# Weights written along the columns by ScalarE ahead of VectorE's multiply, in the joint stage of a graph network

## The reference, cut to what matters

```python
edge_index = jnp.stack([src, dst])
x = _layernorm(x + _L0_gnn_ref(x, edge_index, edge_attr_64, ...), axis=-1)
x = _layernorm(x + _L1_gnn_ref(x, edge_index, ..., 6250), axis=-1)
x = _layernorm(x + _L2_gnn_ref(x, edge_index, ...), axis=-1)
x = _layernorm(x + _L3_gnn_ref(x, edge_index, edge_weight, ...), axis=-1)

# in _L0: messages = relu(concat([x[src], edge_attr]) @ W1.T + b1) @ W2.T + b2
#         agg = segment_sum(messages, dst)
# in _L1, _L2: norm = dis[src] * dis[dst];       segment_sum(x[src] * norm, dst)
# in _L3:      norm = dinv[src] * w * dinv[dst]; segment_sum((x @ W)[src] * norm, dst), three times
```

## Time and profile before

| | |
|---|---|
| median of 3 runs | 5592.74 us (5584.71 to 5594.79) |
| the profiled execution's own time | 5637.0 us |
| its span | 5635.2 us |
| PE, DVE, ACT, POOL busy, share of the span | 85%, 44%, 21%, 21% |
| joint stage, from the first eviction to the last | 134 to 2080 us |
| granted TensorE clock, mean | 0.91 |

### The profile page before, as it was taken

One profiled execution on the slowest core, in us unless ns is written; L12 is line 12 of the kernel. 1 busy time (PEld: TensorE's weight loads), 2 busy tenths in 40 slices (PEclk: granted clock), 3 DMA queues, 4 the chain that ended last, 5 costly groups with the idle time before them and its releaser, 6 DMA issues. The chain is left out here.

```text
span 5635.2 us, 75975 instructions
## 1 busy us (share of the span) xinstructions
PE 4813.6 (85%) x30664; PEld 3047.7 (54%) x30664; DVE 2493.0 (44%) x4225; ACT 1157.3 (21%) x2219; POOL 1199.1 (21%) x845
## 2 busy tenths in 40 slices
PE   3788888888888863388879989999999999999999
PEld 2777777777777753233334444444444444454444
DVE  5877888888788767755542220111000000001111
ACT  0555555555555541100000000000000000000000
POOL 2655656566666610000000000000000000000000
PEclk6888988889898876689989999999999999999999
DMA  4665666666666651288876658887444444338887
GB/s 139 204 199 188 218 198 202 205 202 216 199 213 213 201 179 55 94 299 294 298 225 206 212 187 305 305 306 263 150 155 144 147 149 155 140 132 289 310 306 261
DMA packets 689173, 1178.49 MB, mean 209 GB/s; under 512 B 77284, under 2 KB 450384, under 8 KB 688440
## 3 DMA queue, kind: packets, MB, share of 16 engines
q1 hardware_dynamic: 617004, 1079.58, 55.6%
q0 software_dynamic: 26864, 55.10, 3.9%
q10 hardware_dynamic: 44956, 38.94, 2.2%
HBM read 823.64 MB, written 349.75 MB: 208 GB/s over the span
## 5 line engine op out<-in xcount | busy, mean ns | idle before, releaser
L756 POOL DMA_INDIRECT x<-p_table,src_i x832 | 1191.9, 1433 | 801.6 <-DVE x L553 516.3
L1197 PE MATMUL po_l3b<-mat_l3b,rows_b 128*128 128x512 f32 (+1 forms) x2548 | 1042.5, 569 | 12.2 <-DMA mat_l3b<-weights_fwd 12.2
L740 ACT CAST st_cnt<-ps_mat 128x512 bf16<-128x512 f32 x1225 | 661.2, 585 | 749.4 <-PE ps_deg L665 373.4
L1197 PEld LDWEIGHTS po_l3b<-mat_l3b,rows_b 128*128 128x128 f32 x2548 | 467.6, 191 | 555.7 <-issue 542.4
L675 PE MATMUL ps_mat<-rows_a,hot_s 128*128 128x128 bf16 x7203 | 593.0, 240 | 100.1 <-issue 45.9
L660 PE MATMUL ps_mat<-rows_a,hot_s 128*128 128x128 bf16 x2401 | 396.5, 231 | 230.1 <-issue 81.4
L675 PEld LDWEIGHTS ps_mat<-rows_a,hot_s 128*128 128x128 bf16 x7203 | 482.5, 109 | 162.9 <-ACT st_wt L744 83.2
L1197 PE MATMUL po_l<-mat_l,rows_a 128*128 128x512 bf16 (+1 forms) x1911 | 429.6, 387 | 152.2 <-DVE mat_l L1365 152.2
L541 DVE TENSOR_TENSOR rows_a<-rows_a,slots 128x1536 bf16<-128x1536 bf16 (+1 forms) x294 | 543.5, 1885 | 2.4 <-issue 0.2
L1197 PE MATMUL po_l3a<-mat_l3a,rows_a 128*128 128x512 f32 (+1 forms) x1274 | 523.5, 570 | 16.2 <-DMA mat_l3a<-weights_fwd 16.2
L1197 PE MATMUL po_l3c<-mat_l3c,rows_a 128*128 128x512 f32 (+1 forms) x1274 | 522.1, 569 | 11.8 <-DMA mat_l3c<-weights_fwd 11.7
(11 more groups left out here) (334 smaller groups left out, 4777.3 us busy)
## 6 DMA issues: line engine op xcount, KB each, us to landing
weights_fwd<-st_wt SPq DMA_DIRECT2D x588, 256.0 KB
mat_l<-counts_fwd SPq DMA_DIRECT2D x168, 896.0 KB, 5.4
mat_l3a<-weights_fwd SPq DMA_DIRECT2D x84, 1792.0 KB, 7.1
mat_l3b<-weights_fwd SPq DMA_DIRECT2D x84, 1792.0 KB, 7.1
mat_l3c<-weights_fwd SPq DMA_DIRECT2D x84, 1792.0 KB, 7.1
counts_fwd<-st_cnt SPq DMA_DIRECT2D x588, 128.0 KB
counts_rev<-st_cnt SPq DMA_DIRECT2D x588, 128.0 KB
rev_l<-counts_rev SPq DMA_DIRECT2D x84, 896.0 KB, 7.9
```

The lines of the kernel that those rows point to most:

```text
L740: nc.scalar.copy(st_cnt[:, q, :, j * 2 * P:j * 2 * P + n_col], ps_mat[:, f % 3, :].rearrange("p (d c) -> p d c", d=2)[:, :, 0:n_col]).then ...
L756: pool.indirect_dma_start(ring[:, j % RING, t * FD:(t + 1) * FD], None, p_table, bass.IndirectOffsetOnAxis(src_i[:, j * TH + t:j * TH + t ...
L1197: mm = nc.tensor.matmul(po[:, g % 2, k, 0:nb * P].rearrange("p (d c) -> p d c", c=P), rows[:, s, k * P:(k + 1) * P], mat[:, n % slots, 0:n ...
```

## The change

A new semaphore `spread_w` counts planes. ACT gets a function `weights_along(u, h, v)`: it waits until the unit's slots are there and the half's one-hots of the unit before are used up, and copies plane v of the weights, read with step 0, along the 128 columns of each pair into `hot_w`, which is 128 x 1792 elements for the first half and 128 x 1536 for the second. DVE waits for the plane and multiplies it in place by `hot_d`. On ACT the copies for (u, 1) stand ahead of the evictions of blocks 1, 2 and 3 of unit u, those for (u+1, 0) ahead of the evictions of blocks 9, 10 and 11 of unit u, and those of (0, 0) ahead of everything in the stage.

```diff
@@ one_hots, DVE @@
                         dve.wait_ge(hot_d_ready, m + 1)
                         for v in range(3):
-                            V.tensor_tensor(hot_w[:, h, v, 0:n, :], hot_d[:, h, 0:n, :],
-                                            per_row(slots[:, u % 2, 2 + v, ks], P), ALU.mult).then_inc(hots_ready, 1)
+
+                            dve.wait_ge(spread_w, 3 * m + v + 1)
+                            V.tensor_tensor(hot_w[:, h, v, 0:n, :], hot_w[:, h, v, 0:n, :], hot_d[:, h, 0:n, :],
+                                            ALU.mult).then_inc(hots_ready, 1)
                             tick()
@@ the stage's block of ACT @@
+                    def weights_along(u, h, v):
+                        n = 2 * HALF if h == 0 else NK + 1 - 2 * HALF
+                        act.wait_ge(slots_ready, 2 * u + 1)
+                        if u:
+                            act.wait_ge(filled, (u - 1) * FILLS + (3 * HALF if h == 0 else FILLS))
+                        nc.scalar.copy(hot_w[:, h, v, 0:n, :], per_row(slots[:, u % 2, 2 + v, 2 * HALF * h:2 * HALF * h + n], P)
+                                       ).then_inc(spread_w, 1)
+
+                    for v in range(3):
+                        weights_along(0, 0, v)
                     for n in range(UN):
                         (u, s), q = divmod(n, SUBS), n % STAGES
                         w = sub_cols(s)
+
+                        if 1 <= s <= 3:
+                            weights_along(u, 1, s - 1)
+                        if 9 <= s <= 11 and u + 1 < NB:
+                            weights_along(u + 1, 0, s - 9)
                         for j, k in enumerate(sub_pairs(s)):
```

More of the change, by code:

```diff
@@ L412, in build @@
             sorted_, sort_read, slots_ready = sem("sorted"), sem("sort_read"), sem("slots_ready")
-            hot_d_ready, source_ready = sem("hot_d_ready"), sem("source_ready")
+            hot_d_ready, source_ready, spread_w = sem("hot_d_ready"), sem("source_ready"), sem("spread_w")
             hots_ready, filled, evicted = sem("hots_ready"), sem("filled"), sem("evicted")
```

## The result

The changed kernel takes 5812.7 us (median of 4 runs, 5803.7 to 5813.8) against 5593.8 us for the one before (4 runs, 5584.7 to 5605.1): a ratio of 1.0387, 95% interval 1.0365 to 1.0408. It is 219 us slower. What follows of the traces is about those 167 us.

The account below looks back on a forecast made before the run. No engine is full, so waits decide: PE waits for DVE's one-hots and ACT's evictions. First half -7, second half +88, clock +40 give +121 us: median 5592.7 to 5714 us; own range 5640 to 5810, 8 in 10 5560 to 5840.

Parts of the forecast that it names:

- the second half's terms: Blocks 9 to 11: ACT's copies overshoot its idle time by 1.8 us a unit, +88 us; clock term +40 us.
- the first half's: Up to the 8th block: 14 units start it 1.2 us later, 35 start it 0.7 us earlier, -7 us.
- The operations: DVE's multiplies fall to 1093 and 960 ns; ACT's six planes a unit take 1616 and 1410 ns, 418 us in all.
- Who pays for ACT's time: ACT's copies ahead of evictions in blocks 1 to 3 and 9 to 11 overshoot idle time by 1.2 and 1.8 us.
- rival (a): Joint stage: ACT's idle time absorbs the planes, leaving DVE's gain of about 60 us, 5533 us; chance 0.20.
- rival (c): DVE's multiply does not get faster, so DVE sets the 8th block as before: +145 us, 5738 us; chance 0.10.
- The gain at the 8th block: Start of a unit's second half: PE's waits for DVE's one-hots shrink, worth 65 us at most.
- that same slack: DVE's idle time before L494, waiting for ranks, 5.0 us a unit; message sums slide a few us inside it.
- The clock: Joint stage's granted clock falls from 0.87 to 0.84, PE's 1607 us grow by 57 us, 40 us taken.
- Rival (b): Joint stage: ACT's idle time is no cover, each copy counts in full, 353 us, 5946 us; chance 0.07.
- The rule on multiplies: Skill page's rule putting elementwise multiplies on VectorE, not ScalarE; taken as speaking against the change, with no number.

Follow-up runs that it names:

- e1_old_multiply: Changed kernel with ScalarE's planes kept, but VectorE overwrites them by the old step-0 multiply: 5807 us, 1.0331 of the kernel before.
- e2_no_planes: Kernel before with a dense multiply of the one-hots by themselves, no planes, weights left out: 5709 us, 1.0153 of before.
- e6: Kernel before with no planes and each dense multiply of the one-hots by themselves made twice: 5602 us, 0.9969 of before.
- e8: Kernel before with a dense multiply, no planes, weights left out and GpSimd's gathers left out: 5175 us, 0.9205 of before with gathers.
- e7: Kernel before with GpSimd's gathers left out, their semaphores counted up at once: 5374 us, 0.9557 of before with gathers.
- e9: Changed kernel with GpSimd's gathers left out, their semaphores counted up at once: 5479 us, 1.0163 of the kernel before with its gathers.
- third set: Three runs on one chip, kernel before 5388 us there: changed kernel without gathers (1.0163), kernel before with paced gathers (0.9996), changed kernel with paced gathers (1.0223).
- e12_pause_paced: Kernel before with only the second half's planes, ahead of block 0, dense multiply in that half, gathers paced: 5535 us, 0.9872 of before.
- e5_ranks_pause: Kernel before with only the second half's planes, all three ahead of block 0, dense multiply in that half: 5680 us, 1.0114 of before.
- e10_before_paced: Kernel before with each gather held back until a given number of PE's fills is evicted: 5388 us, 0.9996 of before.
- e11_after_paced: Changed kernel with each gather held back until a given number of PE's fills is evicted: 5518 us, 1.0223 of before.

## Why the prediction was right, and where its sum was not

Slower was right, and so was the range (5560 to 5840 us). The forecast was 121 us and the change cost 219; the forecast's own range, 5640 to 5810, is missed by 3 us. By the parts of a unit, clock included, the first half (blocks 0 to 6) grew by 47 us where the sum had -7, and the second with the ranks by 129 us where it had 88 and 40 for the clock. So the second half's terms came out, and the first half's failed, as far as the clock's share in each can be left aside.

- *The operations.* The multiplies fell as worked out. The planes were 84 and 91 ns longer each: 25 us in all, which the range held and the sum didn't.
- *Who pays for ACT's time.* Right in kind: idle time used up, PE waiting at evictions, rival (a) out. In size the two stretches of planes grew by 2.2 and 0.8 us where I had 1.2 and 1.8, nearly the sum that I gave them; that the errors cancel is luck. For the planes without any gain of VectorE's the sum is that of rival (c), 145 us, and e1_old_multiply cost 1.0331, 185 us on 5594.
- *The gain at the 8th block.* This step failed. The prediction counted DVE's head start as worth up to 65 us on the path and set it against the first half ("14 x 1.2 - 35 x 0.67 = -7 us"), which makes it worth 24 us in the sum (145 - 121). In the changed kernel it is worth nothing (e1_old_multiply; 219 us against 185, across chips, it even costs 34), and alone it costs 86 us (e2_no_planes). Part of the 65 us was misread as well: the 14.2 us behind L533 stand in blocks 8 and 9, where PE already had the half's one-hots. The wait itself did go, as foreseen; its time came back in blocks 7 and 8, 1.3 us a unit longer: PE's idle time in them grew by 43 us, its waits behind evictions of counts most of all, and its clock fell from 0.83 to 0.78. Late fills are in the changed kernel not what grew there: with first evictions they are 159 us in these two blocks before and 154 after (203 in e2_no_planes).
- *What an early engine sets off.* I had written of the message sums that "they slide by a few us inside that same slack" and looked at them as something that could come late. What they did by coming early, and what POOL did by running faster, I didn't price. The sign stood in the trace of before: ACT's 182 us of "remote" waits, and 127 us of PE's waits without a releaser, of which I named 81.4 (the other 45.9 are at L675). I priced neither. Most of the change's loss is the planes'; but this is what turned the expected gain round: VectorE early costs 86 us with gathers (e2), nothing once its time is given back (e6), and gains 199 us without gathers (e8 against e7).
- *The clock.* I took 0.84 and it was 0.84, but of the 57 us that this gives I counted 40 as visible; PE's busy time rose by 108 us. Why by more than the mean clocks give is not shown.
- *Rival (b)*, each plane in full, was nearer to the truth where nothing else disturbs: 304 us between e8 and e9 (across two chips, for 407 us more work of ACT), against its 353.
- *The rule on multiplies.* I took a rule that multiplies belong on VectorE as speaking against the change. The change leaves the multiplies on VectorE and gives ScalarE copies, so it doesn't bear on it.

Open: why fills come late. The runs show that it is PE's signal that is late, that it takes gathers (none without them, e7 and e8, on a chip that took 5620 us with them), that it isn't the gathers alone (none on the chip of the third set), and that dense gathers and late fills go together in time. Leaving the gathers out takes away GpSimd's instructions, their transfers and the waits of POOL and VectorE on each other at once; no run parts these. That the gathers' pitch is the cause was argued, and e12_pause_paced speaks against it as the whole cause. By what path an early VectorE makes more fills late, through GpSimd's gathers or through its own message sums, is argued too. Whether place or pacing makes e12's gain is also open, since no run had the one without the other on its chip.

## What to carry to other kernels

Before moving work between engines, ask of the engine that is relieved what it will release sooner, and into what; here 250 us less work on VectorE cost 86 us. Work put in front of evictions is largely paid when PE has only three banks between itself and them, whatever the engine's idle share over the stage says: 304 us for 407 us of work, where nothing else disturbed. Whether it is cheaper where PE does something that needs no eviction is a fair thing to try; e5_ranks_pause leaves it open. Read "remote" and unnamed waits against the times at which the semaphore was counted up, before pricing anything that stands near them. And take away a suspect (here the gathers) early, in both kernels: it told more than five variants of the change.

## What the runs showed of the hardware that I had not expected

- PE's semaphore updates can come up to 6 us after the last matmul of the fill (6.2 us in the example), in nine of the eleven traces with indirect gathers, and in none of the three without them. The two others, e10_before_paced and e11_after_paced, come from one chip: there the kernel before took 5388 us, and 5594 to 5625 us in the four other sets of runs.
- A GpSimd gather of 128 rows takes 0.94 us while VectorE does nothing and 1.84 us beside its two-input operations; the average over the stage is 1.43 us before and 1.19 us after, with shorter multiplies.
- A bf16 multiply with one operand at step 0 takes 2018 ns for 1792 columns, the dense one in place 1095 ns; a ScalarE copy of a step-0 bf16 operand 1700 ns.
- The clock granted over the joint stage was 0.84 in e2_no_planes and 0.99 in e8_no_planes_no_gathers, which differ in the gathers alone (and ran on two chips); PE's busy time for the same number of matmuls differs by 244 us.
